# A graph kernel on one core: 40 instead of 38 target blocks of layers two and three through the count matrix

## What is computed

```python
h = relu(layernorm(x))
msg = h[dst] @ W_i + h[src] @ W_j + edge_attr @ W_e          # layer one
x = x + segment_sum(edge_weight * msg, dst) + h @ W_self
h = relu(layernorm(x))
def sage(h, Wl, bl, Wr):                                      # layers two and three
    mean = segment_sum(h[src], dst) / max(count(dst), 1)
    return mean @ Wl.T + bl + h @ Wr.T
h = relu(sage(h, W1_l, b1_l, W1_r))
x = x + log_softmax(sage(h, W2_l, b2_l, W2_r))
```

## Time and profile before

| | us |
|---|---|
| median of three runs | 1550.66 (1547.23 to 1553.08) |
| the profiled execution | 1547.76 |
| its span, first to last instruction | 1544.8 |
| granted TensorE clock, mean | 0.943 |

### The profile page before, as it was taken

How to read it: one execution, slowest core, us unless ns; L and a number is a source line. 1 busy time by engine, 2 the same in 40 slices (tenths; PEclk the granted TensorE clock), 3 DMA queues, 4 the chain that set the end, 5 groups by cost and what they waited for, 6 DMA issues and landing times. The chain is left out here.

```text
span 1544.8 us, 27421 instructions
## 1 busy us (share of the span) xinstructions
PE 1218.4 (79%) x9615; PEld 991.2 (64%) x9615; DVE 1048.9 (68%) x2113; ACT 713.1 (46%) x1202; POOL 1076.7 (70%) x1048
## 2 busy tenths in 40 slices
PE   0057888898888889888876498798998888979887
PEld 0035777677777777767754277677776666757665
DVE  7659577988888788877787265455454555666565
ACT  3124344655556445544677143343343443434344
POOL 4877776777777777776777637777774077777770
PEclk9998999999999999999999599999999999989999
DMA  8358555756576466654577556566565665665663
GB/s 248 99 153 234 138 169 165 216 149 190 162 218 176 141 180 191 185 140 131 186 213 226 160 141 196 161 174 187 157 178 146 181 193 149 188 190 161 182 171 88
DMA packets 320573, 266.98 MB, mean 173 GB/s; under 512 B 32393, under 2 KB 298020, under 8 KB 320436
## 3 DMA queue, kind: packets, MB, share of 16 engines
q1 hardware_dynamic: 272708, 189.44, 41.9%
q0 software_dynamic: 33616, 69.34, 17.2%
q10 hardware_dynamic: 14112, 6.43, 1.5%
HBM read 212.08 MB, written 53.00 MB: 172 GB/s over the span
## 5 line engine op out<-in xcount | busy, mean ns | idle before, releaser
L845 POOL DMA_INDIRECT Dt<-h_d,idx x624 | 628.3, 1007 | 200.7 <-issue 188.7
L1451 POOL DMA_INDIRECT Dg<-g_d,idx x390 | 418.3, 1072 | 204.3 <-issue 147.0
L1412 PE MATMUL pc<-Kt,hi 128*128 128x512 f32 (+1 forms) x980 | 397.9, 410 | 13.7 <-issue 6.0
L1412 PE MATMUL pc<-Kt,lo 128*128 128x512 f32 (+1 forms) x980 | 380.5, 392 | 0.0
L1345 DVE CAST Kt<-Ut 128x2048 fp32r<-128x2048 uint8 (+3 forms) x168 | 235.7, 1410 | 55.0 <-PE pc L1412 46.3
L1240 ACT ACTIVATE Cb<-pc 128x784 uint8<-128x784 f32 x304 | 240.2, 823 | 49.6 <-PE pc L1228 47.3
L1412 PEld LDWEIGHTS pc<-Kt,hi 128*128 128x128 f32 x980 | 192.0, 196 | 55.5 <-issue 16.6
L1412 PEld LDWEIGHTS pc<-Kt,lo 128*128 128x128 f32 x980 | 191.8, 196 | 32.2
L1347 ACT ACTIVATE Kt<-Ut 128x1536 fp32r<-128x1536 uint8 (+3 forms) x112 | 181.5, 1622 | 62.6 <-PE pc L1412 52.9
L1202 DVE TENSOR_TENSOR Jt<-ps,keyT 128x1568 bf16<-128x1568 bf16 x204 | 196.5, 969 | 4.5 <-PE pc L1228 1.4
L1228 PE MATMUL pc<-Jt,Rt 128*128 128x196 bf16 x1216 | 148.2, 251 | 41.8 <-ACT Cb L1240 34.6
(11 more groups left out here) (152 smaller groups left out, 1552.3 us busy)
## 6 DMA issues: line engine op xcount, KB each, us to landing
Ut<-c_d SPq DMA_DIRECT2D x126, 448.0 KB, 3.9
Dt<-in_ea SPq DMA_DIRECT2D x208, 192.0 KB
c_d<-Cb SPq DMA_DIRECT2D x38, 784.0 KB
Dq<-in_ea SPq DMA_DIRECT2D x77, 192.0 KB
Dt<-h_d,idx POOLq DMA_INDIRECT x624
g_d<-ht ACTq DMA_DIRECT2D x98, 64.0 KB
r_d<-rt SPq DMA_DIRECT2D x98, 64.0 KB
sp<-g_d SPq DMA_DIRECT2D x14, 448.0 KB, 4.4
```

The lines of the kernel that those rows point to most:

```text
L845: e.indirect_dma_start(Dt[:, s, t, 0:128], None, h_d, bass.IndirectOffsetOnAxis(idx[:, c:c + 1], 0))\
L1412: last = e.matmul(pc[:, k % 2, 0:n], part[:, q, :], Kt[:, t % NK, j - q0, 0:n], start=(x == 0 and t % 2 == 0 and j == 0 and part is hi), s ...
L1451: e.indirect_dma_start(Dg[:, s, t, :], None, (g1_d, g2_d)[L], bass.IndirectOffsetOnAxis(idx[:, c:c + 1], 0)).then_inc(s_gg[s], 16)
```

## The change

One constant:

```diff
-BG = 38
+BG = 40
```

## The result

The changed kernel takes 1563.76 us (median of four, 1560.9 to 1565.15), the kernel before 1548.95 beside it; the ratio is 1.0093, 95% interval 1.0069 to 1.0117. So it is 14 us slower, by more than the 0.5% set as the bound. The profiled execution took 1564.04 us, with a span of 1562.1; it is the pair of profiled executions that differs by 17.3 us in the table, the medians by 14.8.

What follows compares the result with a forecast made beforehand. It took PE, DVE and ACT to set layer one's pace up to about group 41, and POOL's gathers most of layers two and three; 14 + 2.5 = +16.5 us gave 1566 us, range 1545 to 1579.

Steps and rivals of the forecast that it cites:

- Layer one's end hangs on the full ring near group 38: Layer one: PE frees the gather ring near group 38, then 11 groups of POOL follow; added counts cost 14 us.
- The slack at group 49: Layer one: PE waits 10.25 us at group 49, put down to a late gather; least cost 2.4 us.
- What follows moves unchanged: After layer one: the 28.14 us until POOL's next gather move with layer one's end unchanged.
- The first 13 folds keep their places: Layers two and three: these folds stand at the same clock places, so PE's waits of 20.6 and 29.9 us stay.
- Behind the thirteenth fold: Layers two and three: +6.3 us of PE work each, less waits of 6.7 and 3.2: -0.4 and +3.1 us.
- The matmul's price: Layers two and three: a matmul of 512 columns is followed after 0.23 us; wider chunk adds 11.0 us a layer.
- Gathers set the pace: Rival, layers two and three: gathers set the pace, so fewer pull everything forward; 1518 to 1540 us, chance 0.10.
- The added counts vanish: Rival, layer one: added counts disappear in gaps, costing 0 to 5 us; whole 1553 to 1558, chance 0.25.
- Layer one costs more: Rival: each added part costs its whole 1.26 us pitch, plus new cast waits; +24 us, 1575, chance 0.15.
- The signs: Listed observations in all three layers, such as later folds and fewer gather waits, to show the forecast right or wrong.

Runs made afterwards that it cites:

- the counts alone: Kernel before with plain counts of 40 blocks built, 38 used: 1568.23 us against 1549.94, ratio 1.0117; 0.9985 on a chip where before took 2112.92.
- they alone: Changed kernel with plain counts of 38 blocks, the last chunk reading those of blocks 34 to 37: 1543.65 us against 1548.77, ratio 0.9969.
- PACE: Changed kernel with PACE 14.5 instead of 12, a layer's fourteen folds spread over its clock: 1510.11 us, ratio to before 0.9765.
- both edits: Changed kernel with WM 3.3 instead of 1.5 and PACE 14.5 instead of 12: 1508.24 us, ratio to before 0.9719.

## Why the prediction was right, and where its terms were off

The direction and the place held. That the size came out so close, +16.5 us forecast and +14 to +15 measured, is in part luck: of its two terms the one for layer one was too small (14; the counts alone cost 18.3) and the one for layers two and three too large (+2.5; they alone gave -5), and the errors cancel. Step by step:

*Layer one's end hangs on the full ring near group 38.* Right: POOL's last wait for PE is at group 41 in both kernels. Forecast 14 us, measured 17.4 at POOL's last gather (18.0 less 0.6 that POOL's first gather came later). The term that was mis-sized is what is tied to the group number and not to the counts: I took 4 us for a group, from the plain stretch. The formula is for group 38, and its fold came 18.6 us later (19.2 less 0.6). That leaves 20.6 - 18.6 = 2.0 us for 1.29 groups, 1.5 us each. It is no finer than the places of the folds, which shift with the added parts: the fold of group 37 came 23.6 us later, that of group 39 16.7. The other estimate, 16 parts at 0.79 us, was low too: one part costs 1.09 us (17.4 / 16), between DVE's own time and the whole pitch of 1.26 that stood as the upper bound. Taking a value between 12.6 and 15.4 averaged two figures that were both low.

*The slack at group 49.* Misread in part, as said above: some of PE's 10.25 us stood for a load of layer two. It entered only the lower bound of 2.4 us.

*What follows moves unchanged.* Right: 28.39 us instead of 28.14.

*The first 13 folds keep their places.* Right in the main. From the first fold to the thirteenth it is 193.8 us instead of 196.1 in layer two and 200.3 instead of 199.9 in layer three. By the letter, the prediction's own sign of being wrong (closer together than 16.3 us) came in layer two: 16.15 us instead of 16.34, which is 2.3 us in all, and so a small part of the -5. But "20.6 and 29.9 us stay" was wrong: 18.5 and 18.1 were left. POOL's pace is the same, so other things fill the time: PE's busy time in both layers rose by 13.4 us (554.0 to 567.4; the forecast had 14.2), and PE's waits for the copy of a chunk (L1607 on `aT`) went from 0.7 to 7.2 us. A wait at a fixed place is what is left over; it can shrink with no gain.

*Behind the thirteenth fold.* Forecast -0.4 and +3.1, measured -3.6 (86.3 to 82.7) and +2.2 (76.2 to 78.4). The windows from the thirteenth fold on, layer two, first of the kernel before, then of the changed one:

```profile
1127.50:1213.80 86.30, 77.08 (x448) 61.79 (x448) 43.62 (x64) 32.76 (x50) 39.66 (x38) 0.96 0.58 159
...
1144.10:1226.90 82.80, 82.19 (x406) 67.38 (x406) 45.84 (x58) 36.34 (x49) 1.81 (x2) 0.96 0.54 148
```

The granted clock is 0.96 in both. PE's busy time rose by 5.1 us, where the forecast had 6.3, and its idle time fell from 9.2 to 0.6, by 8.6, where it had 6.7: with the gathers' wait went shorter ones (2.0 us for ACT before L1122, now 0.5). In layer three the busy time rose by 4.1 (69.0 to 73.1) and the idle time fell by 1.9 (7.2 to 5.3) instead of 3.2, since a wait of 3.2 us for a cast stands where 2.0 stood. So the added work was priced too high in both, and what becomes of PE's other waits when one is removed was not asked.

*The matmul's price.* 0.23 us for 512 columns held: it is the median start to start in the changed kernel too, and the busy time rose by 13.4 us against a forecast of 14.2. The 131 ns of the Trainium skill ("TensorE: Matmul & The Clock Gate", Back-to-back issue gap) is not seen in this kernel.

*The rivals.* "Gathers set the pace" fell: by the rule of the Trainium skill ("Perfetto Trace Analysis", What "DMA-bound" means) POOL's solid track was the bound, and 72 gathers fewer, 98 us of them, brought 5 us. It was near the truth in one thing: the waits that it counted were worth 50 us to whoever moves the folds, as `PACE` showed; the change itself doesn't. "The added counts vanish" fell with the counts alone. "Layer one costs more" had the nearer of the two prices of a part: 1.26 us, where 1.09 was measured and 0.79 stood in the forecast.

*The signs.* The range held, but most of what was to show it came in another size: the folds behind group 30 were 9 to 24 us later (10 to 15 named), POOL's waits for PE rose by 19.8 us (10 to 15), its last gather was at 900.7 (897), layer two took 314 us (319), the waits for gathers fell by 23.8 us (about ten), and layer three took 5.5 us more by its window (2 to 4). The long last stretch of dense work came as named.

## What to carry to other kernels

When two engines keep pace through a ring, find the last place where the ring is full and ask what the change does there: slack behind it (PE's 10 us at group 49) does not pay for work in front of it. Work taken from the engine that the chain names gains little (here 5 us for 98) while the places at which the other engine meets it stay where they are; the change and the schedule have to move together (here one constant more was worth 50 us). A wait of TensorE can cost more than its length: look at the granted clock behind it. And where steps of the next stage stand in an engine's fixed order, look at what they wait for: idle time that looks like slack can be theirs.

## What the runs showed of the hardware

Not expected: removing 29.9 us of PE's waits, none longer than 5.0 us, took away another 23 us of PE's busy time, as stretches at 1.2 instead of 2.4 GHz went. Folds at 1.51 us instead of 0.86 stand behind idle times of PE (4.96 us in the row above, 2.54 to 6.66 in layer two of the kernel before), though not each such wait has one, and with no wait for gathers above 1.5 us the granted clock was 1.00 over the whole of layer two. It is not the gathers alone: with both edits layer three was granted 0.96 and PE waited for no gather in it. The Trainium skill ("TensorE: Matmul & The Clock Gate", Loop structure matters more than you think) says that the loop nest decides whether matmuls stay at full clock; here moving the folds within the same loops changed it too, by the trace.

And the same program took 1549 us on some chips and 2109 to 2113 on others, with VectorE and ScalarE instructions of unchanged length, more idle time between them, and a granted TensorE clock of 0.80 instead of 0.98 in the stretch above. Its cause is open. In two pairs of runs, the ratio carried over where it was large (0.9765 and 0.9736 for the spread folds), and not where it came from a narrow margin (1.0117 and 0.9985 for the counts alone).
